# A two-layer feature-interaction kernel on one core: VectorE folds the weights ahead of the products of units 1 and 2, and rows are transposed later

## What is computed

```
e[b, m, :] = tbl_m[ids[b, m]]                       # (512, 32, 64)
x1 = einsum('oc,bcd->bod', W0, e (x) e) + b0        # W0 (128, 32*32)
x2 = einsum('oc,bcd->bod', W1, e (x) x1) + b1       # W1 (128, 32*128)
z  = concat(x1.sum(2), x2.sum(2))                   # (512, 256)
h  = relu(concat(z, dense_ctx) @ W_top1 + b_top1)
y  = relu(h @ W_top2 + b_top2) @ W_top3
```

## Time and profile before

| | us |
|---|---|
| median of 3 runs (lowest, highest) | 204.75 (202.44, 205.6) |
| the profiled execution, its own time | 203.88 |
| its span, first to last instruction | 202.1 |
| PE busy | 183.8 (91%) |
| ACT busy | 146.9 (73%) |
| DVE busy | 142.8 (71%) |
| POOL busy | 124.3 (62%) |

### The profile page before, as it was taken

One profiled execution on the slowest core, in us unless ns is written; L12 is line 12 of the kernel. 1 busy time (PEld: TensorE's weight loads), 2 busy tenths in 40 slices (PEclk: granted clock), 3 DMA queues, 4 the chain that ended last, 5 costly groups with the idle time before them and its releaser, 6 DMA issues.

```text
span 202.1 us, 8905 instructions
## 1 busy us (share of the span) xinstructions
PE 183.8 (91%) x3815; PEld 157.7 (78%) x3815; DVE 142.8 (71%) x381; ACT 146.9 (73%) x370; POOL 124.3 (62%) x134
## 2 busy tenths in 40 slices
PE   6875999987849989999999999999999999999775
PEld 6765999966728857877888887688889879889674
DVE  2228579999763599999997768999864797671200
ACT  2465988766797598899796779979677788756423
POOL 3777777887777777777777777777777760000000
PEclk9999999999985999999999999999999999999999
DMA  5981111111114314535411411141141113010100
GB/s 163 339 307 27 29 26 29 24 29 24 27 31 82 74 35 92 90 115 144 75 29 26 81 29 29 31 81 31 29 80 31 31 31 57 0 23 14 25 4 0
DMA packets 16520, 12.26 MB, mean 61 GB/s; under 512 B 12513, under 2 KB 12897, under 8 KB 16482
## 3 DMA queue, kind: packets, MB, share of 16 engines
q1 hardware_dynamic: 12242, 7.44, 14.6%
q0 software_dynamic: 4096, 4.20, 11.8%
q10 hardware_dynamic: 144, 0.07, 0.1%
HBM read 9.59 MB, written 0.00 MB: 47 GB/s over the span
## 4 chain that ended last, share of the span: by engine, by line
PE 66%; ACT 12%; DVE 7%; DMA 6%; issue 5%; SPq 2%; ACTq 0%; DVEq 0%
PE psum L448 21%; PE psum L217 14%; ACT t_sb L258 8%; PE psum L326 5%; DMA t_sb<-w0x 5%; PE psum L534 4%; PE psum L187 4%; PE psum L516 4%; PE psum L328 3%; DVE prod L285 3%; DVE t_sb L254 3%; PE psum L400 2%; PE psum L505 2%; PE psum L202 2%; PE psum L315 2%
## 5 line engine op out<-in xcount | busy, mean ns | idle before, releaser
L615 POOL DMA_INDIRECT rows<-table,idx x128 | 123.6, 966 | 40.8 <-issue 38.4
L285 DVE TENSOR_TENSOR prod<-psum,xx 128x512 f32<-128x512 f32 (+2 forms) x224 | 89.9, 472 | 21.2 <-issue 9.0
L258 ACT ACTIVATE t_sb<-psum 64x308 f32<-64x308 f32 (+1 forms) x184 | 78.3, 425 | 18.1 <-PE psum L217 12.1
L448 PE MATMUL psum<-coef,t_sb 128*64 128x128 f32 (+1 forms) x954 | 54.1, 276 | 0.5 <-DMA t_sb<-t_sb 0.5
L448 PEld LDWEIGHTS psum<-coef,t_sb 128*64 128x64 f32 (+1 forms) x954 | 47.7, 132 | 4.1 <-issue 3.2
L217 PE MATMUL psum<-prod,xx 64*32 64x154 f32 x1920 | 43.3, 301 | 5.6 <-DVE t_sb L254 2.4
L217 PEld LDWEIGHTS psum<-prod,xx 64*32 64x32 f32 x1920 | 31.0, 107 | 13.4 <-issue 10.1
L254 DVE COPY t_sb<-psum 64x308 f32<-64x308 f32 x60 | 28.8, 481 | 8.2 <-PE psum L217 7.1
L710 ACT ACTIVATE coef<-psum 128x320 f32<-128x320 f32 (+1 forms) x43 | 18.9, 486 | 3.2 <-PE psum L328 1.0
L710 ACT ACTIVATE t_sb<-psum 128x212 f32<-128x212 f32 x25 | 10.8, 544 | 9.3 <-PE psum L315 9.3
L347 DVE TENSOR_TENSOR t_sb<-t_sb,coef 128x64 f32<-128x64 f32 (+6 forms) x70 | 16.2, 303 | 0.2
(11 more groups left out here) (39 smaller groups left out, 119.1 us busy)
## 6 DMA issues: line engine op xcount, KB each, us to landing
rows<-table,idx POOLq DMA_INDIRECT x128
t_sb<-t_sb SPq DMA_DIRECT2D x28, 64.0 KB, 2.6
w_sb<-w1t SPq DMA_DIRECT2D x3, 512.0 KB, 7.4
t_sb<-w0x SPq DMA_DIRECT2D x1, 768.0 KB, 10.3
w0g_sb<-w0g SPq DMA_DIRECT2D x1, 512.0 KB, 9.5
w_sb<-top SPq DMA_DIRECT2D x2, 256.0 KB
w_sb<-top SPq DMA_DIRECT2D x1, 512.0 KB
w_sb<-w1t SPq DMA_DIRECT2D x1, 384.0 KB, 5.0
```

The lines of the kernel that those rows point to most:

```text
L258: copy_t(act, lambda o, i: act.activation(o, i, ACT.Copy), 0, u, v)
L285: return dve.tensor_tensor(at(p, col, out), at(psum, XT[g] * BANK + a, first), at(x, x0 + b, second), ALU.mult)
L448: return pe.matmul(bank(ACC, half * O, O, j, width), t_sb[:, c:c + width], w, start=i < places, stop=i >= n - places, tile_position=(0, j))
L615: pool.indirect_dma_start(rows[:, c:c + D], None, table[:, :], bass.IndirectOffsetOnAxis(ap=idx[:, g:g + 1], axis=0))\
```

## The change

- VectorE copies the pair products x = 1, 4, ... 28 (ten; before seven). Its addition that prepares the cross products' input comes after x = 22, and the products of unit 0 come after its last pair copy.
- The rows of unit 0 are transposed after pair product 28 and before cross product 1, those of unit 1 before cross products 10 and 15, half 2,0 after coefficient group 10, and half 2,1 between the two halves of unit 1.
- VectorE makes the products of unit 1 after all folds, and those of unit 2 after its copies of unit 1.
- ScalarE makes all 14 coefficient copies; VectorE in exchange copies the upper 64 partitions of all four groups of unit 1 (before: of two).
- In units 2 and 3 (the contraction of block 0) each part of `contract` comes ahead of `t_half` and `transpose_rows`.

```diff
--- before.py
+++ after.py
@@ -153,11 +153,11 @@
 
 
 
-        PAIR_BY = [int(x in (1, 4, 7, 10, 17, 20, 23)) for x in range(M)]
+        PAIR_BY = [int(x % 3 == 1 and x < 30) for x in range(M)]
         CROSS_BY = [0] * M
         W_BY = PAIR_BY + CROSS_BY
         V_GROUPS = -(-VCOLS // 4)
-        COPIER = [0] * 8 + [n % 2 for n in range(8, V_GROUPS)]
+        COPIER = [0] * V_GROUPS
         FOLD_NEAR, FOLD_ALL = 10, 12
         TOP_DMAS = 6
 
@@ -172,7 +172,7 @@
             return u // UNITS % 2 * COLS * CHUNK + u % UNITS * UNIT
 
         def copier(group, p):
-            return int(p == 1 and (group % 2 == 1 if group < 4 * (ALL - 1) else group % 4 > 1))
+            return int(p == 1 and (group % 2 == 1 if 8 <= group < 4 * (ALL - 1) else group < 8 or group % 4 > 1))
 
         def copied(n, groups):
             return sum(copier(i, p) == n if i // 4 >= NARROW else p == n == 0 for i in range(groups) for p in range(2))
@@ -626,14 +626,14 @@
 
             for x in range(M):
                 pair_product(pe, x)
-                if x in (14, 27):
-                    transpose_rows(pe, 0, (14, 27).index(x))
+                if x == 28:
+                    transpose_rows(pe, 0, 0)
             for x in range(M):
-                if x in (4, 13):
-                    transpose_rows(pe, 1, (4, 13).index(x))
+                if x == 1:
+                    transpose_rows(pe, 0, 1)
+                if x in (10, 15):
+                    transpose_rows(pe, 1, (10, 15).index(x))
                 cross_product(pe, x)
-                if x in (22, 31):
-                    transpose_rows(pe, 2, (22, 31).index(x))
             pe.wait_ge(u_copied[0], W_BY.count(0))
             pe.wait_ge(fills_ready, 1)
             for v in range(4):
@@ -642,17 +642,23 @@
                 if n == C_BANKS.index(TG):
                     pe.wait_ge(t_copied[0], copied(0, 3))
                 transpose_coef(pe, n)
+                if n == 10:
+                    transpose_rows(pe, 2, 0)
             for n in range(2):
-                pe.wait_ge(coef_ready[n], COPIER.count(n))
+                wait(pe, coef_ready[n], COPIER.count(n))
             pe.wait_ge(w0g_in_sb, 16)
 
-            for u in range(1, EVEN):
+            t_half(pe, 1, 0)
+            transpose_rows(pe, 2, 1)
+            t_half(pe, 1, 1)
+            for u in range(2, EVEN):
                 b = u // 2 - 1
                 for g in range(2):
+                    if b == 0:
+                        contract(pe, b, 2 * (u % 2) + g)
                     t_half(pe, u, g)
-                    if u > 1:
-                        transpose_rows(pe, u + 1, g)
-                    if b >= 0:
+                    transpose_rows(pe, u + 1, g)
+                    if b > 0:
                         contract(pe, b, 2 * (u % 2) + g)
                     if g == 0 and top_step(u, 7) is not None:
                         l1(pe, top_step(u, 7))
@@ -712,24 +718,27 @@
             act.dma_start(at(t_sb, base_in, [[1, idx.shape[1]]]).bitcast(I32), base).then_inc(ids_in_sb, 16)
 
             for x in range(M):
-                if x in (17, 30):
-                    act_xx(act, 0, (17, 30).index(x))
-                    act_gram(act, 0, (17, 30).index(x))
+                if x == 30:
+                    act_xx(act, 0, 0)
+                    act_gram(act, 0, 0)
                 if PAIR_BY[x] == 0:
                     copy_pairs(act, plain, x)
             for x in range(M):
-                if x in (6, 15):
-                    act_xx(act, 1, (6, 15).index(x))
-                    act_gram(act, 1, (6, 15).index(x))
+                if x == 3:
+                    act_xx(act, 0, 1)
+                    act_gram(act, 0, 1)
+                if x in (12, 17):
+                    act_xx(act, 1, (12, 17).index(x))
+                    act_gram(act, 1, (12, 17).index(x))
                 copy_cross(act, plain, x)
             for g in range(2):
                 act_copy_t(act, 0, 2 * g)
                 act_copy_t(act, 0, 2 * g + 1)
-                act_xx(act, 2, g)
-                act_gram(act, 2, g)
             for n in range(V_GROUPS):
-                if COPIER[n] == 0:
-                    copy_coef(act, plain, n)
+                copy_coef(act, plain, n)
+                if n == 10:
+                    act_xx(act, 2, 0)
+                    act_gram(act, 2, 0)
 
             act.wait_ge(bias_ready, 1)
             def copies(u, g):
@@ -740,13 +749,15 @@
                 act_xx(act, u, g)
                 act_gram(act, u, g)
 
-            for u in range(1, EVEN):
+            copies(1, 0)
+            fields_in(2, 1)
+            copies(1, 1)
+            for u in range(2, EVEN):
                 if u % 2 == 0 and u >= 4:
                     copy_acc(act, plain, u // 2 - 2)
                 for g in range(2):
                     copies(u, g)
-                    if u > 1:
-                        fields_in(u + 1, g)
+                    fields_in(u + 1, g)
                     if g == 0 and top_step(u, 7) is not None:
                         l1_relu(act, top_step(u, 7))
                     if g == 1 and top_step(u, 7) is not None:
@@ -807,17 +818,16 @@
             for x in range(M):
                 if PAIR_BY[x] == 1:
                     copy_pairs(dve, dve.tensor_copy, x)
-                if x == 10:
+                if x == 22:
                     dve.wait_ge(w0x_in_sb, 16)
                     n = 4 * QUART * WIDE_Z
                     dve.tensor_tensor(at(t_sb, w0x_at, [[1, n]]), at(t_sb, cross_in, [[1, n]]),
                                       at(t_sb, cross_in + n, [[1, n]]), ALU.add).then_inc(w0_ready, 1)
-                    products(dve, 0, 0)
+            products(dve, 0, 0)
             products(dve, 0, 1)
             dve.wait_ge(ident_ready, 1)
             dve.tensor_tensor(stack[1][:, :], ident[:, 0:2 * UNIT], ident[:, 2 * UNIT:4 * UNIT], ALU.add)\
                 .then_inc(stack_ready, 1)
-            products(dve, 1, 0)
             dve.wait_ge(stack_ready, 1)
             dve.tensor_tensor(stack[0][:, :], stack[1][:, 0:UNIT], stack[1][:, UNIT:2 * UNIT], ALU.add)\
                 .then_inc(stack_ready, 1)
@@ -827,7 +837,6 @@
             fold_near(dve, 0, False)
             dve.wait_ge(fold_step, 1)
             fold_near(dve, 0, True)
-            products(dve, 1, 1)
             copied_w(dve, 2 * QUART)
             fold_near(dve, 1, False)
             dve.wait_ge(fold_step, 3)
@@ -846,18 +855,17 @@
             fold_far(dve, 1, False)
             dve.wait_ge(fold_step, 11)
             fold_far(dve, 1, True)
+            products(dve, 1, 0)
+            products(dve, 1, 1)
+            for v in range(4):
+                dve_copy_t(dve, 1, v)
             products(dve, 2, 0)
-            for n in range(V_GROUPS):
-                if COPIER[n] == 1:
-                    copy_coef(dve, dve.tensor_copy, n)
             products(dve, 2, 1)
 
-            for u in range(1, ALL - 1):
+            for u in range(2, ALL - 1):
                 for g in range(2):
-                    if u >= NARROW:
-                        dve_copy_t(dve, u, 2 * g + 1)
-                    if u > 1:
-                        products(dve, u + 1, g)
+                    dve_copy_t(dve, u, 2 * g + 1)
+                    products(dve, u + 1, g)
             copy_acc(dve, dve.tensor_copy, 7)
             dve_copy_t(dve, ALL - 1, 2)
             dve_copy_t(dve, ALL - 1, 3)
```

## The result

| | before | changed |
|---|---|---|
| median, us (22 runs each) | 203.37 | 201.49 |
| lowest to highest | 201.12 to 206.67 | 199.18 to 204.2 |
| ratio, 95% interval | | 0.9919 [0.9891, 0.9948] |
| profiled execution, its time and span | 203.88, 202.1 | 203.31, 201.1 |

The changed kernel is 0.8% faster, clear of the noise and under 2%. The forecast was 201.4, in the range, with the right sign. The comparison that gives a ratio leaves out the longest runs, here and in the experiments, and of before more than of some variants, so a ratio can lie above the quotient of the medians.

A forecast was written before the change was run, and what follows sets the result against it. TensorE's pauses in head and filling were taken as where time can go, with VectorE and TensorE nearly equally loaded in the steady part. -4.0 + 0 + 1.1 + 0.4 = -2.5 from 203.88 gave 201.4 us, range 198.0 to 204.3.

The forecast's parts named there:

- Step A: Pair and cross products: two TensorE holes and two row transposes go, so unit 0 starts at 37.1; 4.0 us gained.
- Step B: VectorE's folds: they end at 42.1 to 42.4, before TensorE wants them; 0 us, bounds -0 and +0.6.
- The hole: TensorE pause of 1.66 us in unit 0's matmuls, ascribed to the instruction stream and kept; bounds -1.66 and 0.
- Step C: Coefficient copies by ScalarE alone: transposes to unit 1 take 8.4 us, not 7.3; +1.1 us, bounds 0 and 1.5.
- Step D: Pipeline filling, unit 1 to half 3,1: VectorE's chain plus an expected slow-clock stretch; +0.4 us, bounds -1.1 and +1.8.
- at full clock that is -1.1: Filling stage: VectorE's 18.4 us from unit 1 to half 3,1, set against 19.5 before.
- Step E: Beyond half 3,1: the shift is kept, since the self-scheduled gather keeps slack; 0 us, upper bound +0.5.
- Signs of being wrong: Cross products pausing for ScalarE, folds setting transposes' start, clock down over 8 us, end moving less than half 3,1's start.
- The clean head: Rival: unit 0's 1.66 us pause is hidden or vanishes and the clock stays up in filling; 198.2 us, chance 0.17.
- VectorE taking it back: Rival: VectorE without slack from unit 1's start to 100 us eats 2.4 of the gain; 203.8 us, chance 0.15.
- The slower case, by the clock: Rival: idle time ahead of unit 1 starts a longer slow-clock stretch, +4.7 against the forecast; 206.1 us, chance 0.08.

The follow-up runs named there:

- experiment 1: Kernel before with only the new pair-copy split, late addition, later products (0,0) and (0,1), and moved row transposes of units 0 and 1; ratio 1.002 to before, median 202.2 us.
- experiment 4: Changed kernel with ten warm-up matmuls of 128 columns replaced by three of 512, 28 TensorE instructions fewer; ratio 0.9938 to before, median 201.11 us.
- experiment 9: Changed kernel with its ten warm-up matmuls turned into sixteen of 80 columns, 24 TensorE instructions more, no fills; ratio 1.0184 to before, median 207.86 us.
- experiment 10: Changed kernel with TensorE pauses filled by seven unused matmuls and two 512-column warm-up matmuls, 4 instructions fewer in all; ratio 0.9832 to before, median 199.87 us.
- Experiment 3: Changed kernel with VectorE copying coefficient groups 10 and 12 in place of ScalarE; ratio 0.9878 to before, median 199.52 us.
- experiment 8: Kernel before with TensorE pauses filled by unused matmuls ahead of unit 1, between its halves and ahead of half 2,0; ratio 1.0174 to before, median 205.72 us.
- experiment 2: Changed kernel with block 0's contraction parts put back behind half and transpose in units 2 and 3; ratio 1.0026 to before, median 202.18 us.
- experiment 11: Changed kernel with VectorE copying coefficient groups 10 and 12, pauses filled by six unused matmuls, and two 512-column warm-up matmuls; ratio 0.9838 to before, median 199.78 us.
- experiment 12: Changed kernel with VectorE copying coefficient groups 10 and 12 and two 512-column warm-up matmuls, no fills; ratio 0.9822 to before, median 199.72 us.

## Why the prediction was right, step by step

- **Step A (-4.0): right.** Unit 0 at 37.08, forecast 37.1.
- **Step B (0): right for the changed kernel** (folds end at 42.3, forecast 42.1 to 42.4; group 0 waits for the hole, not for the folds), but "folding costs nothing" hides what it earns: without it unit 1 starts no earlier than before (experiment 1).
- **The hole (kept): right,** 1.51 for 1.66, and that it belongs to the stream of instructions is shown: its place followed the count in experiments 4, 9 and 10, each time to the matmul. Its length varies, and goes down to 0.56 (experiment 9). The Trainium skill (Runtime: NRT & Kernel Launch, Instruction fetch mechanics) has the block of 256 instructions, and the marks 256 apart agree; that a crossing is mostly hidden doesn't hold in unit 0, where a pair of weight load and matmul takes 16 ns.
- **Step C (+1.1): right in kind, 0.3 too high.** From the transposes to unit 1 it is 8.1 us, 7.3 before: +0.8. Experiment 3 gives VectorE two copies back, where three had moved, for 1.0.
- **Step D (+0.4): the sum near, the working wrong.** Half 3,1 at 71.25, forecast 71.4; the slow stretch came and lasted 6.8 us. From unit 1 to half 3,1 it is 20.3 us, 19.5 before: +0.8 and not +0.4. (The slow stretch of before ends at 65.8, where the prediction read 65.6.) But "at full clock that is -1.1" set 18.4 at full clock against 19.5 of a stretch with slow clock. At equal clock it is 18.8 (experiment 4) against 16.9 (experiment 8, with fills; 17.3 in experiment 1, without): +1.9. So the order alone gives 3.4 - 1.9 = 1.5 us, which is what the spans at clock 1.00 show (199.35 against 197.8); the times show 1.2 (201.2 against 200.0). Also wrong: "the transposes put behind contractions only change order". Together with the contraction ahead of the half, that order keeps TensorE from standing 4.2 us (experiment 2), and is worth 0.7 us of the median, mostly by way of the clock.
- **Step E (0): mis-sized, this is where forecast and result part.** In the profile half 3,1 starts 2.6 us earlier and the span ends 1.0 earlier. A shift isn't kept just because nothing absolute stands behind it: a second slow stretch took 1.7 us (2.9 gained at half 4,0, 1.2 at half 4,1), behind the 1.67 us pause ahead of half 4,0 that was in none of my rows. The pause as such costs nothing: experiment 4 has it too, and at full clock half 4,1 starts there 8.3 us behind half 3,1, 8.5 in the kernel before. Another 0.5 went at 149 us, at half 12,0, in a gap of the weight loads that no semaphore explains. And 0.37 is lost outside the span. By the ratio the change is worth 1.65 us (0.0081 of 203.37), where the sum had 2.5.
- **Signs of being wrong.** Two that I had named came true in the profile: the clock was down for 10.2 us and not 8 (6.8 and 3.4), and the end moved by less than the start of half 3,1.
- **Luck in the number.** 201.4 lies 0.1 from the median of 201.49. The sum started from 203.88, and the median of before came out as 203.37. So 0.5 of the 0.85 us by which the gain was forecast too large doesn't show in the time; the rest is that ratio and medians weigh the runs differently. And that half 3,1 came out within 0.15 us of the forecast is in part the errors of steps C and D, which offset each other.
- **Rivals.** The clean head occurs as the runs at clock 1.00, but gives 200.0 and not 198.2: the hole is still there at full clock (1.39 us in two parts in experiment 4, where -1.7 was forecast), and step D has the error above. VectorE taking it back didn't come as forecast: the gain of 2.6 us at half 3,1 is 2.9 at half 4,0. What VectorE's longer chain takes is the 1.9 of step D. The slower case, by the clock, was seen as a mechanism in experiments 1 and 2, though not in the changed kernel's median. That pauses bring the clock down in the filling stage is supported by experiments 10 and 11 (11 of 13 runs at clock 1.00, against 8 of 34 of the unfilled changed kernel, and 3 of 18 in experiments 4 and 12, which have no fills and a warm-up of three or two long matmuls). A pause doesn't decide it alone: the profile of 4 has these pauses, that of 12 the one of 1.67, and both have full clock. That a single named pause does it wasn't tried.

Open: what adds 0.37 us outside the span, and that the transfer of instructions is what delays the last pack. The wait goes with the count of instructions (nine kernels with no more than before, four with 20 to 28 more), and in the trace the transfer stands amid the pack's packets (seen), but no run changed the transfer alone.

## What to carry to other kernels

Compare spans only at the same granted clock: take the price of a stage from a profile in which the stage ran at full clock, and count by runs how often it does. When work is moved out of an engine's wait, follow it to the next place where that engine has none left, and put independent work (here a contraction) ahead of the waiting step. In an unrolled kernel like this one, with short matmuls, the number of instructions is a tuning parameter: with 24 more at the start, the wait at the end grew by 1.2 us. Compare span and time too: a part of a launch lies outside its span, and can differ between two kernels.

## What the runs showed of the hardware

- A stream of 32-column weight loads and 77-column matmuls (256 pairs in 4.03 us) stops for 0.6 to 1.8 us, at a place set by the count of instructions, and a second stop comes 128 pairs behind the first (experiments 4 and 10). It seems to outrun the supply of instructions.
- A wait of 2.0 us near the end was followed by 6.8 us at half clock (experiment 8): from the last contraction's last part to the end it took 12.7 us, and 9.6 in the kernel before, whose wait of 0.53 at the same place left the clock alone.
- A gather on GpSimd takes 944 ns, but up to 2,281 while VectorE folds (two SBUF inputs), and 940 to 947 while it makes products (one input from PSUM). The Trainium skill (SBUF — State Buffer, Who interferes with whom) has VectorE instructions with two SBUF inputs contend with GpSimd instructions that read SBUF, and those with at most one, outside the 2-port modes, not, and the trace agrees. It cost nothing here, since gathers run ahead.
